# A Mamba layer and a top-2 expert layer on one core: the DMA queue's order in the blocks, and the router's casts

## The reference

```python
# 1: selective scan (inner width 512, 16 states), reduced
xp, res = split(x @ W_in.T)
xc = silu(causal_conv4(xp) + conv_b)
B, C, z = split(xc @ W_x.T)                  # 16, 16, 1
dt = softplus(z @ W_dt.T + b_dt)
h = exp(A * dt) * h + dt * B * xc            # per token and state
y = silu((h * C).sum(states) + D * xc + res) @ W_out.T
x = layernorm(x + y)
# 2: router over 8 experts, the two best
p = softmax(x @ router_w.T); w, e = top_k(p, 2); w = w / (w.sum() + 1e-9)
out = sum_k w[k] * (gelu(x @ w1[e[k]].T + b1[e[k]]) @ w2[e[k]].T + b2[e[k]])
x = layernorm(x + out)
```

## Time and profile before

| What | Value |
|---|---|
| median of 3 runs | 1548.41 us (1547.02 to 1553.11) |
| profiled execution, its own time | 1544.33 us |
| its span, first to last instruction | 1542.7 us |
| blocks of the scan (first to last scan) | 55 to 943 us |
| expert stage and combination | from about 1000 us |
| mean granted TensorE clock | 0.935 of full speed |

### The profile page before, as it was taken

How to read it: one execution, slowest core, us unless ns; L and a number is a source line. 1 busy time by engine, 2 the same in 40 slices (tenths; PEclk the granted TensorE clock), 3 DMA queues, 4 the chain that set the end, 5 groups by cost and what they waited for, 6 DMA issues and landing times. The chain is left out here.

```text
span 1542.7 us, 29244 instructions
## 1 busy us (share of the span) xinstructions
PE 1340.7 (87%) x8828; PEld 1119.7 (73%) x8829; DVE 1153.1 (75%) x2010; ACT 1013.4 (66%) x1370; POOL 1036.7 (67%) x981
## 2 busy tenths in 40 slices
PE   4698898998998898998898898199999999999960
PEld 1377677777677677677677687189999999999860
DVE  5678888888988888988877887656666666666546
ACT  4898998979978978978987883234334334433324
POOL 3478787779878878878988998635444444444336
PEclk8699999999999999999999998599999999999985
DMA  7012223222322222322321326421453612311027
GB/s 262 21 56 86 72 65 102 69 87 73 91 86 75 91 84 75 104 70 76 103 73 59 110 76 225 138 74 53 149 167 110 217 41 85 119 38 42 25 70 275
DMA packets 85568, 150.12 MB, mean 97 GB/s; under 512 B 11042, under 2 KB 34210, under 8 KB 85476
## 3 DMA queue, kind: packets, MB, share of 16 engines
q1 hardware_dynamic: 70228, 116.39, 23.6%
q0 software_dynamic: 9888, 27.29, 5.3%
q10 hardware_dynamic: 5360, 5.26, 1.0%
HBM read 104.45 MB, written 44.45 MB: 97 GB/s over the span
## 5 line engine op out<-in xcount | busy, mean ns | idle before, releaser
L1327 POOL TENSOR_TENSOR arena<-arena 128x1024 f32<-128x1024 f32 x256 | 604.1, 2370 | 32.0 <-DVE arena L1021 17.0
L465 PE MATMUL d_ps<-ident,arena 128*128 128x128 f32 x2048 | 331.2, 287 | 59.3 <-DVE arena L1021 56.7
L465 PEld LDWEIGHTS d_ps<-ident,arena 128*128 128x128 f32 x2048 | 248.6, 147 | 177.5 <-issue 89.5
L1021 DVE TENSOR_TENSOR_SCAN arena<-arena,carry,d_ps 128x512 f32<-128x512 f32 x256 | 316.5, 1268 | 49.9 <-PE d_ps L465 47.1
L1021 DVE TENSOR_TENSOR_SCAN arena<-arena,d_ps 128x512 f32<-128x512 f32 x256 | 301.9, 1208 | 63.8 <-PE d_ps L465 61.1
L756 ACT ACTIVATE arena<-u_tok,b_tok 128x512 f32<-128x512 f32 x508 | 324.7, 714 | 5.6 <-PE d_ps L465 4.0
L478 PE MATMUL y_ps<-ident,arena 128*128 128x128 f32 x2048 | 301.8, 278 | 7.3 <-POOL arena L1327 7.3
L1663 ACT ACTIVATE h_t<-ht_ps 128x512 f32<-128x512 f32 x142 | 84.4, 595 | 295.9 <-PE ht_ps L1718 295.9
L774 ACT ACTIVATE arena<-dt,neg_a 128x2048 f32<-128x2048 f32 x128 | 255.5, 1996 | 2.1 <-DVE neg_a L1255 1.1
L478 PEld LDWEIGHTS y_ps<-ident,arena 128*128 128x128 f32 x2048 | 244.0, 144 | 8.5 <-POOL arena L1327 8.2
L1728 PEld LDWEIGHTS y_ps<-arena,h_parts 128*128 128x128 f32 x1704 | 214.6, 193 | 9.0 <-issue 4.2
(11 more groups left out here) (220 smaller groups left out, 1712.4 us busy)
## 6 DMA issues: line engine op xcount, KB each, us to landing
arena<-c_rows SPq DMA_DIRECT2D x128, 256.0 KB
arena<-weight_parts SPq DMA_DIRECT2D x20, 1024.0 KB, 5.3
weight_parts<-arena SPq DMA_DIRECT2D x64, 256.0 KB, 3.7
xg<-expert_rows POOLq DMA_DIRECT2D x71, 130.0 KB
arena<-in_pieces SPq DMA_DIRECT2D x16, 512.0 KB, 8.7
arena<-in_pieces SPq DMA_DIRECT2D x64, 128.0 KB, 3.5
arena<-expert_out SPq DMA_DIRECT2D x16, 512.0 KB, 9.8
weight_parts<-arena SPq DMA_DIRECT2D x4, 1024.0 KB, 5.0
```

Of the source, the lines that this page charges most:

```text
L465: last = nc.tensor.matmul(d_ps[:, c % 2, j * P:(j + 1) * P], ub[:, g % U_RING, j, c * P:(c + 1) * P], t.ident[:], start=True, stop=True, i ...
L1021: nc.vector.tensor_tensor_scan(h[:, g % H_RING, c, :], decay[:, g % D_RING, c, :], d_ps[:, c % 2, :], 0.0 if i % 2 == 0 else carry[:, n, c ...
L1327: nc.gpsimd.tensor_tensor(h[:, g % H_RING, lo:hi, :], h[:, g % H_RING, lo:hi, :], c_row[:, g % C_RING:g % C_RING + 1, :].broadcast_to([P, ...
```

## The change

In the queue of SyncE: the raw piece is no longer issued behind the store of the piece before it. It is issued in the step after its own slot's store, a step sooner than now (`fetch`). The residual's x moves from step 4 to step 6, the x tile of block i + 2 from step 7 to step 9, each with its wait.

In the router: the three casts of `router_pick` become reductions over a single element. TensorE also writes the row of expert numbers into the logits' bank, by one more matmul with the identity, and the compare reads it from there. The bank is thus freed by the compare, no longer by the copy of the logits, and GpSimd's `router_member` waits for that. In `router_place` VectorE only reduces. The cast to an integer, and the last block's wait for earlier sends, move to GpSimd, ahead of the first row that it sends.

```diff
-                nxt = k - 1 + PARTS_RING
-                if k >= 1 and nxt < PARTED:
-                    sp.wait_ge(parts_stored[nxt % PARTS_RING], 16 * (nxt // PARTS_RING))
+
+            def fetch(k):
+                if k < PARTED:
+                    sp.wait_ge(parts_stored[k % PARTS_RING], 16 * (k // PARTS_RING))
                     hold(sp, held_sp)
-                    sp.dma_start(parts[:, nxt % PARTS_RING, 1], raw_piece(nxt))\
-                        .then_inc(raw_loaded[nxt % PARTS_RING], 16)
+                    sp.dma_start(parts[:, k % PARTS_RING, 1], raw_piece(k)).then_inc(raw_loaded[k % PARTS_RING], 16)
...
+                    piece = piece_of(*divmod(g - 2, STATE))
+                    if piece is not None:
+                        fetch(piece + PARTS_RING)
                     piece = piece_of(*divmod(g - 1, STATE))
                     if piece is not None:
                         hand_on(piece)
-                    if n == 4 and back:
+                    if n == 6 and back:
...
-                    if n == 7 and early and scans:
+                    if n == 9 and early and scans:
...
                     if j == TT - 1:
+                        last = nc.tensor.matmul(bank("logits", p)[:, TT * EXPERTS:(TT + 1) * EXPERTS], t.ident[:],
+                                                t.iota_ef[:], start=True, stop=True)
                         last.then_inc(m_filled[bank_of("logits", p)], 1)
...
                     nc.vector.tensor_copy(logit[:].rearrange("p j e -> p (j e)"),
-                                          bank("logits", p)[:, 0:TT * EXPERTS])\
-                        .then_inc(m_freed[bank_of("logits", p)], 1)
-                    wait_freed(dve, "logits", p)
+                                          bank("logits", p)[:, 0:TT * EXPERTS]).then_inc(picked, 1)
+                    dve.wait_ge(picked, 4 * p + 1)
...
-                    nc.vector.tensor_copy(rows_of(p)[:, :, DIM + 1], idx[:, :, 0])
-                    nc.vector.tensor_copy(rows_of(p)[:, :, DIM + 3], t.token2[:, p, :])
-                    nc.vector.tensor_copy(ek[:], idx[:, :, 0:TOPK]).then_inc(picked, 1)
                     dve.wait_ge(picked, 4 * p + 3)
+                    nc.vector.tensor_reduce(rows_of(p)[:, :, DIM + 1], idx[:, :, 0:1], AXX, ALU.add)
+                    nc.vector.tensor_reduce(rows_of(p)[:, :, DIM + 3], t.token2[:, p, :].unsqueeze(2), AXX, ALU.add)
+                    nc.vector.tensor_reduce(ek[:], idx[:, :, 0:TOPK].unsqueeze(3), AXX, ALU.add).then_inc(picked, 1)
+                    dve.wait_ge(picked, 4 * p + 4)
                     nc.vector.tensor_tensor(
                         onehot[:].rearrange("p j k e -> p (j k) e"),
-                        t.iota_ef[:].unsqueeze(1).broadcast_to([P, TT * TOPK, EXPERTS]),
+                        bank("logits", p)[:, TT * EXPERTS:(TT + 1) * EXPERTS].unsqueeze(1)
+                        .broadcast_to([P, TT * TOPK, EXPERTS]),
                         ek[:].rearrange("p j k -> p (j k)").unsqueeze(2).broadcast_to([P, TT * TOPK, EXPERTS]),
-                        ALU.is_equal).then_inc(picked, 1)
+                        ALU.is_equal).then_inc(m_freed[bank_of("logits", p)], 1)
...
                     dve.wait_ge(spread, p + 1)
-                    if p == BLOCKS - 1:
-                        dve.wait_ge(rows_sent[p % 2], 16 * TT * TOPK * (p // 2))
+                    dve.wait_ge(place_chain, p)
                     nc.vector.tensor_reduce(rk[:], onehot[:], AXX, ALU.add).then_inc(pos_done, 1)
-                    dve.wait_ge(pos_done, 2 * p + 1)
-                    nc.vector.tensor_copy(pos[:, p % 2], rk[:]).then_inc(pos_done, 1)
-                    dve.wait_ge(pos_done, 2 * p + 2)
...
-                    pool.wait_ge(pos_done, 2 * b + 2)
+                    pool.wait_ge(pos_done, b + 1)
+                    if b == BLOCKS - 1:
+                        pool.wait_ge(rows_sent[b % 2], 16 * TT * TOPK * (b // 2))
+                    nc.gpsimd.tensor_copy(pos[:, b % 2], rk[:]).then_inc(place_chain, 1)
+                    pool.wait_ge(place_chain, b + 1)
...
-                    pool.wait_ge(picked, 4 * p + 4)
+                    wait_freed(pool, "logits", p)
```

More of the change, by code:

```diff
@@ L1110, in router_pick @@
                     last.then_inc(picked, 1)
-                    dve.wait_ge(picked, 4 * p + 1)
+                    dve.wait_ge(picked, 4 * p + 2)
                     hold(dve, held_dve)
@@ L1115, in router_pick @@
                     last.then_inc(picked, 1)
-                    dve.wait_ge(picked, 4 * p + 2)
-                    nc.vector.tensor_copy(rows_of(p)[:, :, DIM + 1], idx[:, :, 0])
-                    nc.vector.tensor_copy(rows_of(p)[:, :, DIM + 3], t.token2[:, p, :])
-                    nc.vector.tensor_copy(ek[:], idx[:, :, 0:TOPK]).then_inc(picked, 1)
                     dve.wait_ge(picked, 4 * p + 3)
+                    nc.vector.tensor_reduce(rows_of(p)[:, :, DIM + 1], idx[:, :, 0:1], AXX, ALU.add)
+                    nc.vector.tensor_reduce(rows_of(p)[:, :, DIM + 3], t.token2[:, p, :].unsqueeze(2), AXX, ALU.add)
+                    nc.vector.tensor_reduce(ek[:], idx[:, :, 0:TOPK].unsqueeze(3), AXX, ALU.add).then_inc(picked, 1)
+                    dve.wait_ge(picked, 4 * p + 4)
                     nc.vector.tensor_tensor(
                         onehot[:].rearrange("p j k e -> p (j k) e"),
-                        t.iota_ef[:].unsqueeze(1).broadcast_to([P, TT * TOPK, EXPERTS]),
+                        bank("logits", p)[:, TT * EXPERTS:(TT + 1) * EXPERTS].unsqueeze(1)
+                        .broadcast_to([P, TT * TOPK, EXPERTS]),
                         ek[:].rearrange("p j k -> p (j k)").unsqueeze(2).broadcast_to([P, TT * TOPK, EXPERTS]),
-                        ALU.is_equal).then_inc(picked, 1)
+                        ALU.is_equal).then_inc(m_freed[bank_of("logits", p)], 1)
                 def router_sum(p=p):
```

## The result

The changed kernel takes 1500.99 us (median of 4 runs, 1499.31 to 1502.46), the kernel before beside it 1549.59 (1547.02 to 1553.11). The ratio is 0.9685, 95% interval 0.9661 to 0.9709, so 3.15% faster. I had forecast 1526 us and a range down to 1513. The sign was right, and the gain of 48.6 us was more than twice the 21.3 us that I had added up. The profiled execution of the changed kernel took 1502.46 us (span 1500.8).

What follows compares the result with a forecast made beforehand. TensorE in the scan blocks, idle 86 us there, was taken as nearest to a bound. Queue 15.5, router 4.1 and clock 1.7 summed to 21.3 us, giving 1523 or 1527; forecast 1526 us, own range 1518 to 1536, wider 1513 to 1541.

Steps and rivals of the forecast that it cites:

- TensorE's gap at the turn of u: Step 13, six blocks: TensorE idles 16.3 us until ScalarE copies the turn before; 9.6 us expected back.
- half clock: Half-rate stretches behind step 13 gaps in blocks 3 to 6: one of four expected gone, 1.7 us.
- steps 11 and 12: y_u, taps: Product y_u: second halves gain 4.4 us, first halves lose 1.5; VectorE's wait before a tap in block 0: 3 us.
- pick, block 7, extra matmul: Router pick: net 1.2 us in blocks 2 to 6, 2.5 in block 7, less 0.8 for the extra matmul.
- tail: Router cast moved to GpSimd, on the path twice in the tail at 0.3 us each: −0.6 us.
- the upper end: Step 13, from block 6: without the raw piece wait the copy is 2.2 us earlier, covering its gap; 13 us.
- My lower end: Step 13, from block 4: 0.33 us lateness plus 0.82 us piece wait, 1.15 of 3.04 us; 6.9 us in all.
- rival 2: Clock stays up: all four half-rate stretches go, with step 13's upper ends; gain 29 to 34 us, chance 0.13.
- Rival 1: DMA waits were hidden: only the router's 4.1 us and about 2 us come, 1542 us; chance 0.17.
- rival 3: Router's reduces and compare wait as the casts did: router part −8 us, total gain 9 us, 1539 us; chance 0.07.
- rival 4: x tile comes too late for the in-projection: slower, 1563 us if 10 us late; chance 0.05.
- The other signs of being right: Included raw-piece waits under 10 us, SyncE's gate wait 1 to 3 us a block, GpSimd variance waits in each block.

Runs made afterwards that it cites:

- The fetch alone: Kernel before with only the raw piece fetched a step sooner, x tile's and residual's moves and router edits left out: 1513.46 us, ratio 0.9795.
- the filler run: Kernel before plus 16 unused transposes in TensorE's step 13 gap of blocks 3 to 6: 1538.39 us, ratio 0.9950.
- the repeat: Kernel before run once more, unchanged, for a second profile: 1547.66 us.
- the two runs with extra code: Kernel before plus one unread matmul per block: 1541.55 us, ratio 0.9963; kernel before plus 16 unused matmuls near TensorE's program start: 1539.35 us, 0.9943.

## Why the prediction was wrong

The account of the two profiled executions, 1542.7 to 1500.8 us: the start −0.9, from the first scan to GpSimd's last product −39.4, from there to the first matmul of the expert stage +4.4, the expert stage −5.9. My 21.3 us were almost all meant for the second of these.

| Part | Forecast, us | Measured, us |
|---|---|---|
| TensorE's gap at the turn of u | 9.6 (6.9 to 13) | 13.1 |
| half clock | 1.7 (0 to 6.8) | 12.0 |
| steps 11 and 12: y_u, taps | 5.9 (block 0: 3) | 15.3, some 5 of it clock |
| pick, block 7, extra matmul | 2.9 | 5.3 |
| place, in the blocks | 1.8 | 2.9 |
| tail | −0.6 | −4.4 |
| expert stage | 0 | 5.9 |

The rows sum to some 45 us without the clock counted twice. The rest, −3 us, is in other steps of the blocks, which became longer (steps 0, 1 and 10 by 4.3 us together).

**What bounds the kernel.** Right: TensorE is the one to read, and a wait of ScalarE is not a gain by itself. The sentence that this wait "must not be taken as the gain" led me too low all the same. The fetch alone gained 33.4 us in steps 11 to 13, half of the 67.5 us of waits; I had 17.2 with the clock.

**Step 13 and the steps before it, the first failed step.** I took the middle between two ends, and the upper end was the true one: 13.1 of 16.3 us. My lower end held TensorE's own pace fixed, "ScalarE takes up the last scaling 0.33 us after TensorE's turn of step 12". But TensorE was itself late there because of ScalarE. Timelines of the kernel before, block 4, step 11 to 12, ScalarE and then VectorE and TensorE:

```profile
584.02 0.15 ACT L803 COPY halo<-m_ps 128x3 f32<-128x3 f32 x1
```

```profile
584.89 0.75 DVE L1032 SCALAR_TENSOR_TENSOR pre<-m_ps,conv_w,pre 128x511 f32<-128x511 f32 x1 [0.48 <-ACT pre L804]
```

```profile
588.59 0.66 PE L465 MATMUL d_ps<-ident,arena 128*128 128x128 f32 x4 [0.44 <-DVE arena L1021]
```

ScalarE comes to L803, without a pause before it, 3.1 us after the in-projection that began at 577.65 had ended (580.92). VectorE waits 0.48 us for the tap, and TensorE 0.44 us for VectorE. This chain, ScalarE to tap to scan to drive, stands in the waits of before as 13.8 us for L1032, of which I had used only block 0's 3.04. In the changed kernel it is 8.9. So steps 11 and 12 gained 15.3 us and not 5.9, the larger miss of the two. That TensorE's lateness there had capped the gain of step 13 is my reading of these rows; no run holds one of the two steps fixed.

**y_u.** The second halves went to 1.20 us in blocks 1 to 5, as predicted (4.4 us); that of block 0, which I had not counted, is still at 2.45. The first halves took 1.92, 2.37 and 2.07 us in three of six blocks, an excess of 2.8 us where I had 1.5.

**The clock, the second failed step and the term most wrong.** I knew the price of a stretch (1.7 us) and let one of four go. All four of step 13 went (6.8 us), and with the three in steps 11 and 12 of blocks 0, 2 and 6 it is 23.9 us of half clock, 12.0 us of time. The busy time of TensorE in the blocks agrees, 14.0 us less. I treated the gaps as halved and took most stretches to stay; the gaps shrank to 0.81 us and less. This was my rival 2, with 0.13 and a gain of up to 34 us. It named the right mechanism for the miss in size, and yet stopped short, because it counted only the stretches behind the gaps of step 13. The rule of the Trainium skill that I cited with it ("TensorE: Matmul & The Clock Gate", "HAM oscillation — how this bites in real kernels") is borne out at step 13 by the filler run: TensorE busy, clock 1.00. It does not hold without exception there, as the 3.07 us gap in block 2 of the repeat shows. And that the clock's 12.0 us come from the shorter gaps is shown for the four stretches of step 13 alone.

**The router.** The reduces, the compare from PSUM and the wait at the turn of B came as forecast in size (160 ns, 224 ns, 0.54 us for 0.65). The extra matmul cost more than forecast, 1.3 us in step 5 for 0.8. And I subtracted the wait at the turn of B in full. Steps 6 of blocks 2 to 6 gained 3.9 us against 1.2, so most of that wait lay in time in which TensorE would have waited for the scan. Block 7 gained 2.8 for 2.5. In step 15 of block 7 another 4.6 us show, but GpSimd's products end there, and they gained nothing from it: "I count nothing there" was right. For the tail I had 0.3 us twice. The casts, of which three stand behind the last scan, with the waits behind them and what followed cost 4.4 us, of which 2.8 came back without them; the rest is within the 2 us by which this stretch differs between kernels with the same tail.

**The expert stage.** "No edited line" was true, and the stage still gained 5.9 us, 4.8 of it in one slot: a pause of 3.2 us and 1.6 us of half clock behind it. I had put this stage at nothing on the ground that its code was not touched. The gain came with the extra matmul as more code in TensorE's program, which is shown by the two runs with extra code; why the length of the program matters stays open. None of my rivals had it.

**The others.** Rival 1 (the DMA waits are hidden), rival 3 (the reduces wait) and rival 4 (the x tile late) did not happen. SyncE issued block 4's x tile at 547.37, and it was there 3.7 us later, 5.8 us ahead of the first in-projection (556.89). The other signs of being right came in kind, but not SyncE's wait for the gates, 3.9 us a block where I had written 1 to 3; it costs no time that was measured once the piece is ahead of it, as the fetch alone showed. The residual's x, put at nothing, cost nothing that was measured in the changed kernel.

## What to carry to other kernels

When an engine off the bound is late, follow its lateness to each place where it meets the bound, and do not hold the bound's pace fixed while you cost one of these places: here the same late transfer was paid in three steps. Closing a TensorE gap can also pay in granted clock (12.0 us of half-rate loss went here), so cost both, but do not count on it: the filled gaps gave no gain that could be told. And take the place of TensorE's code as an unknown of some microseconds in a stage behind a loop. Before you trust a gain or a loss under 1% in an unedited stage, pad the program by instructions without effect and look whether it stays.

## What was not expected of the hardware

- One slot behind the loop of the expert stage took 9.9 to 11.7 us with one TensorE program and 6.7 with every longer one, padding of 16 unused matmuls far ahead included.
- A VectorE cast of 128x4 lasted 4.12 us and ended within 0.05 us of a run of two GpSimd products. A GpSimd instruction on 128x4 varied as well: the one at L1383 had a median of 1195 ns in the kernel before and 220 ns at the same place after.
- The total of half clock was the same in two executions of the same kernel (75.1 us twice, 51.2 twice), though single stretches of 3.4 us moved between steps in the first. Over different kernels it lay between 41 and 79 us and was not in order of TensorE's gaps at the turn of u: 41.0 us with 10.2 us of such gaps, 54.6 with 3.3.
- An indirect DMA of GpSimd started 0.86 us after the end of the cast of its positions, whether GpSimd had cast (0.18 us, at 901.36 in the changed kernel) or VectorE (to 941.86 in the kernel before). Where VectorE had written them some 5 us earlier, GpSimd's pause was 0.13 us.
